# Axial attention on one Trainium2 core: maxima and scores on opposite 64 rows of the array, with the PSUM banks dealt out anew

## The reference, cut to what matters

```python
q = (x @ Wq).reshape(b, n, N_HEADS, HEAD_DIM)
k, v = jnp.split(ctx @ Wkv, 2, axis=-1)
...
q = apply_axial_rope(q, pos_map)
k = apply_axial_rope(k, ctx_pos_map)
scale = 1.0 / np.sqrt(HEAD_DIM).astype(np.float32)
logits = jnp.einsum('bqhd,bkhd->bhqk', q, k) * scale
w = jax.nn.softmax(logits, axis=-1)
attn = jnp.einsum('bhqk,bkhd->bqhd', w, v)
attn = attn.reshape(b, n, N_HEADS * HEAD_DIM)
return attn @ Wout + bout
```

## Time and profile before

| | |
|---|---|
| Median of 3 runs | 2910.94 us (2908.63 to 2911.35) |
| The profiled execution | 2908.72 us |
| Its span, first to last instruction | 2906.9 us |
| PE, DVE, ACT, POOL busy | 85%, 62%, 43%, 10% |
| Mean granted TensorE clock | 0.951 of full |
| First and last maxima of the stage | 2023.1 and 2585.3 us |

### The profile page before, as it was taken

How to read it: one execution, slowest core, us unless ns; L and a number is a source line. 1 busy time by engine, 2 the same in 40 slices (tenths; PEclk the granted TensorE clock), 3 DMA queues, 4 the chain that set the end, 5 groups by cost and what they waited for, 6 DMA issues and landing times. The chain is left out here.

```text
span 2906.9 us, 42566 instructions
## 1 busy us (share of the span) xinstructions
PE 2467.0 (85%) x15730; PEld 1904.7 (66%) x15746; DVE 1799.7 (62%) x5199; ACT 1248.9 (43%) x2982; POOL 297.7 (10%) x535
## 2 busy tenths in 40 slices
PE   5889999999974999799999999995888888883674
PEld 4668999998864999476667766763655555551332
DVE  6656767667875666445445544454566666657986
ACT  3434445444433211244344434452544444436663
POOL 3211100001000000000000000002111111101220
PEclk8999999999986999999999999997999999996887
DMA  4101211112005000000000000001000000003001
GB/s 156 62 23 41 70 37 40 69 36 74 29 26 194 1 1 1 1 1 1 1 1 1 1 1 1 1 1 51 5 5 5 5 5 5 5 1 133 1 1 58
DMA packets 41212, 83.41 MB, mean 29 GB/s; under 512 B 4528, under 2 KB 17840, under 8 KB 39856
## 3 DMA queue, kind: packets, MB, share of 16 engines
q1 hardware_dynamic: 41008, 80.70, 7.9%
HBM read 72.30 MB, written 8.39 MB: 28 GB/s over the span
## 5 line engine op out<-in xcount | busy, mean ns | idle before, releaser
L1990 DVE TENSOR_REDUCE s_nmax<-s_a_ps 128x2 f32<-128x512 f32 x256 | 174.3, 686 | 198.7 <-PE s_a_ps L1772 195.7
L651 ACT ACTIVATE s_p<-s_ms,s_nmax 128x256 f32<-128x256 f32 x256 | 128.5, 503 | 192.3 <-DVE s_nmax L754 192.3
L754 DVE CUSTOM_DVE_ANT_0 s_ms<-s_s_ps,s_bias 128x256 f32<-128x256 f32 x256 | 98.2, 421 | 175.9 <-PE s_s_ps L529 175.5
L1375 ACT ACTIVATE l_wo_w<-l_wo_w,s_nmax 128x128 f32<-128x128 f32 (+1 forms) x256 | 114.4, 447 | 197.8 <-DVE s_nmax L1471 197.0
L512 PE MATMUL s_q_ps<-s_xT,s_wh 128*128 128x256 f32 x1024 | 189.6, 286 | 0.0
L1215 PE MATMUL s_s_ps<-l_wqb_w,s_lT 128*128 128x512 f32 x384 | 175.7, 597 | 16.0 <-DVE l_wo_w L1441 15.3
L914 PE MATMUL s_h_ps<-s_xh,s_t 128*128 128x256 f32 x704 | 173.0, 284 | 9.3 <-DVE s_xl L1002 9.3
L1886 ACT ACTIVATE s_pT<-s_s_ps 128x512 f32<-128x512 f32 x256 | 151.6, 606 | 59.6 <-PE s_s_ps L1785 57.3
L562 PE MATMUL s_y_ps<-s_wh,s_oT 128*128 128x512 f32 x512 | 173.0, 399 | 0.0
L914 PE MATMUL s_h_ps<-s_xl,s_t 128*128 128x256 f32 x704 | 172.4, 283 | 0.0
L512 PEld LDWEIGHTS s_q_ps<-s_xT,s_wh 128*128 128x128 f32 x1024 | 165.5, 193 | 6.0 <-issue 0.5
(11 more groups left out here) (304 smaller groups left out, 6686.8 us busy)
## 6 DMA issues: line engine op xcount, KB each, us to landing
s_x_raw<-kept SPq DMA_DIRECT2D x24, 512.0 KB, 3.3
s_c_in<-in_ctx_T SPq DMA_DIRECT2D x32, 256.0 KB, 2.5
l_wqb_w<-in_l_xwq SPq DMA_DIRECT2D x4, 1024.0 KB, 7.8
l_wqb_w<-in_l_xwo SPq DMA_DIRECT2D x4, 1024.0 KB, 10.1
kept<-s_x_raw SPq DMA_DIRECT2D x8, 512.0 KB, 2.7
l_wo_w<-in_l_wo SPq DMA_DIRECT2D x1, 4096.0 KB, 15.5
s_raw<-in_l_w1T SPq DMA_DIRECT2D x2, 2048.0 KB, 9.9
s_raw<-in_l_w2T SPq DMA_DIRECT2D x2, 2048.0 KB, 21.5
```

The lines of the kernel that those rows point to most:

```text
L651: act.activation(p[:, h % PR, q, :], ms[:, h % 2, q, :], ACT.Exp, scale=-1.0, bias=nmax[:, h % PR, q:q + 1], accum_out=den[:, h % PR, q:q ...
L754: dve.tensor_tensor_reduce(ms[:, h % 2, q, :], s_ps[:, h % 2, q * S:(q + 1) * S], bias[:, h // PER % B, :], -SCALE, 3.0e38, ALU.add, ALU.m ...
L1375: act.activation(p[:, h % PR, q, 0:(q + 1) * P], ms[:, h % 2, q, 0:(q + 1) * P], ACT.Exp, scale=-1.0, bias=nmax[:, h % PR, q:q + 1], accum ...
L1990: dve.tensor_reduce(nmax[:, g % 2, :, 2 * pair + e], a_ps[:, n % 2, :].rearrange("p (q k) -> p q k", q=QT), AX_X, ALU.max, negate=True).th ...
```

## The change

The maxima of head n and the scores of head n-11 are now issued in turns, part by part, in `products`, each on the 64 rows in which its head lies. `head_of` puts heads of even number in the upper and of odd number in the lower half, so that the two heads of a step always lie in opposite halves. `kTz` becomes `kT` without the zeros; the two fills go away, and a k is copied out by one instruction. Transpositions follow the products. `t_ps` has one bank, `a_ps` three. `outputs` works on a whole group of eight heads, in steps 5, 13, 21 and 29, ahead of the step's projection, and `pT` holds sixteen heads. The projections move: q from steps 10 and 14 to 8 and 11, v from 12 and 13 to 15 and 16, y from 16 and 18 to 18 and 20; k stays at 19 and 21. The reciprocal moves from step 21 to 22 (and each eighth from there), the scaling from 22 to 23.

```diff
     LAG = GH + 3
-    QUADS = H // 4
-    QUAD_LAG = LAG + 3 + 2
-    OUT_LAG = QUAD_LAG + 5
-    Q_AT, K_AT, V_AT, Y_AT = (10, 14), (19, 21), (12, 13), (16, 18)
+    PV_LAG = LAG + GH + 2
+    OUT_LAG = PV_LAG + 1
+    Q_AT, K_AT, V_AT, Y_AT = (8, 11), (19, 21), (15, 16), (18, 20)
...
-        return n // GH, n % 4, n % GH // 4
+        return n // GH, n % GH // 2, n % 2
...
-        kTz = m.sb("kTz", [P, H, S], F32R)
+        kT = m.sb("kT", [P, H // 2, S], F32R)
...
-        pT = m.sb("pT", [P, GH, QT, S])
+        pT = m.sb("pT", [P, 2 * GH, QT, S])
...
-        t_ps = m.ps("t", [P, 2, 512])
+        t_ps = m.ps("t", [P, 512])
-        a_ps = m.ps("a", [P, 2, 512])
+        a_ps = m.ps("a", [P, 3, 512])
...
-                pe.wait_ge(t_out, at + 1)
+                pe.wait_ge(t_out, at + 2)
...
-                pe.wait_ge(a_out, b * H + n + 1)
-                for q in range(QT):
-                    mm = pe.matmul(a_ps[:, n % 2, q * S:(q + 1) * S], qTx[:, g % 2, pair, q * P:(q + 1) * P],
-                                   kTz[:, GH * g + 2 * pair + e, :], start=True, stop=True)
-                mm.then_inc(a_full, 1)
+                pe.wait_ge(a_out, max(b * H + n, 1))
...
+            def products(b, n, j):
+                for part in range(QT):
+                    if n is not None:
+                        g, pair, e = head_of(n)
+                        rows = slice(XD * e, XD * (e + 1))
+                        mm = pe.matmul(a_ps[:, (b * H + n) % 3, part * S:(part + 1) * S], qTx[rows, g % 2, pair, part * P:(part + 1) * P],
+                                       kT[rows, PAIRS * g + pair, :], start=True, stop=True)
+                        if part == QT - 1:
+                            mm.then_inc(a_full, 1)
+                    if j is not None:
+                        g, pair, e = head_of(j)
+                        rows = slice(XD * e, XD * (e + 1))
+                        mm = pe.matmul(s_ps[:, j % 2, part * S:(part + 1) * S], kT[rows, PAIRS * g + pair, part * P:(part + 1) * P],
+                                       qTm[rows, g % 2, pair, :], start=True, stop=True)
+                        if part == QT - 1:
+                            mm.then_inc(s_full, 1)
+
+            def outputs(b, g):
+                pe.wait_ge(s_out, b * H + 2 + GH * (g + 1))
+                pe.wait_ge(o_out, b * G + g + 1)
+                for e in range(2):
+                    for k in range(QT):
+                        for part in range(2):
+                            for pair in range(PAIRS):
...
             def steps_of(b):
                 for n in range(H):
+                    whose = "prev" if n < LAG else "here"
+                    if has(b, whose):
+                        scores_wait(b, whose, (n - LAG) % H)
                     if has(b, "here"):
-                        greatest(b, n)
+                        greatest_wait(b, n)
+                    products(b, n if has(b, "here") else None, (n - LAG) % H if has(b, whose) else None)
                     for use in t_turns.steps[n]:
...
-                    heads = slice(GH * g, GH * (g + 1), 2)
-                    act.copy(kTz[0:XD, heads, cols], t[0:XD])
-                    heads = slice(GH * g + 1, GH * (g + 1), 2)
-                    act.copy(kTz[XD:P, heads, cols], t[XD:P]).then_inc(t_out, 1)
+                    act.copy(kT[:, PAIRS * g:PAIRS * (g + 1), cols], t).then_inc(t_out, 1)
...
-            act.copy(kTz[0:XD, 1::2, :], blank[0:XD, :].unsqueeze(1).broadcast_to([XD, H // 2, S])).then_inc(fixed, 1)
...
-            dve.tensor_copy(kTz[XD:P, 0::2, :], blank[XD:P, :].unsqueeze(1).broadcast_to([XD, H // 2, S])).then_inc(fixed, 1)
```

More of the change, by code:

```diff
@@ L1726, in rows_over @@
                     pe.wait_ge(x_full, b * G + g + 1)
-                pe.wait_ge(t_out, at + 1)
+                pe.wait_ge(t_out, at + 2)
                 for k in range(4):
-                    to = t_ps[:, bank, k * P:(k + 1) * P]
+                    to = t_ps[:, k * P:(k + 1) * P]
                     if of == "x":
@@ L1768, in greatest, with scores_wait @@
                         pe.wait_ge(t_out, t_turns.at(b - 1, last) + 3)
[L1770 to L1776 removed]
+                pe.wait_ge(a_out, max(b * H + n, 1))
+            def scores_wait(b, whose, n):
                 g, pair, e = head_of(n)
@@ L1783, in scores @@
                 pe.wait_ge(s_out, (b + shift[whose]) * H + n + 1)
-                for k in range(QT):
-                    mm = pe.matmul(s_ps[:, n % 2, k * S:(k + 1) * S], kTz[:, GH * g + 2 * pair + e, k * P:(k + 1) * P],
-                                   qTm[:, g % 2, pair, :], start=True, stop=True)
-                mm.then_inc(s_full, 1)
-            def outputs(b, m):
-                g, e = m // 2, m % 2
-                pe.wait_ge(s_out, b * H + 2 + 4 * m + 4)
-                if e == 0:
-                    pe.wait_ge(o_out, b * G + g + 1)
-                for k in range(QT):
-                    for part in range(2):
-                        for pair in range(PAIRS):
-                            ones_or_values = one[:, e, :] if part else v[:, k, GH * g + 2 * pair + e, :]
-                            mm = pe.matmul(o_ps[32 * pair:32 * pair + 32, part, :], ones_or_values,
-                                           pT[:, 4 * e + pair, k, :], start=(e == 0 and k == 0 and part == 0),
-                                           stop=(e == 1 and k == QT - 1 and part == 1))
+            def products(b, n, j):
[14 more added lines that the diff above has]
+                            mm.then_inc(s_full, 1)
@@ new lines, in outputs @@
+            def outputs(b, g):
[5 more added lines that the diff above has]
+                            for pair in range(PAIRS):
+                                ones_or_values = one[:, e, :] if part else v[:, k, GH * g + 2 * pair + e, :]
+                                mm = pe.matmul(o_ps[32 * pair:32 * pair + 32, part, :], ones_or_values,
+                                               pT[:, GH * (g % 2) + 2 * pair + e, k, :],
+                                               start=(e == 0 and k == 0 and part == 0),
+                                               stop=(e == 1 and k == QT - 1 and part == 1))
@@ L1815, in steps_of @@
                             rows_over(b + shift[use[0]], t_turns.at(b, use), t_turns.bank(b, use), *use[1:])
-                    whose = "prev" if n < LAG else "here"
-                    if has(b, whose):
-                        scores(b, whose, (n - LAG) % H)
-                    whose = "prev" if n < QUAD_LAG else "here"
-                    if n % 4 == QUAD_LAG % 4 and has(b, whose):
-                        if whose == "here" and n == QUAD_LAG:
+                    whose = "prev" if n < PV_LAG else "here"
+                    if n % GH == PV_LAG % GH and has(b, whose):
+                        if whose == "here" and n == PV_LAG:
                             pe.wait_ge(f_out, f_turns.at(b, ("here", "v", QT - 1)) + 2)
-                        outputs(b + shift[whose], (n - QUAD_LAG) % H // 4)
+                        outputs(b + shift[whose], (n - PV_LAG) % H // GH)
                     for use in f_turns.steps[n]:
@@ L1854, in _ @@
                            ACT.Sin).then_inc(sines, 1)
-            act.wait_ge(fixed, 1)
-            act.copy(kTz[0:XD, 1::2, :], blank[0:XD, :].unsqueeze(1).broadcast_to([XD, H // 2, S])).then_inc(fixed, 1)
             def rows_over(at, bank, of, g, q):
                 act.wait_ge(t_full, at + 1)
-                t = t_ps[:, bank, :].rearrange("p (k n) -> p k n", k=4)
+                t = t_ps[:, :].rearrange("p (k n) -> p k n", k=4)
                 cols = slice(q * P, (q + 1) * P)
@@ L1989, in greatest @@
                 dve.wait_ge(a_full, b * H + n + 1)
-                dve.tensor_reduce(nmax[:, g % 2, :, 2 * pair + e], a_ps[:, n % 2, :].rearrange("p (q k) -> p q k", q=QT),
+                dve.tensor_reduce(nmax[:, g % 2, :, 2 * pair + e], a_ps[:, (b * H + n) % 3, :].rearrange("p (q k) -> p q k", q=QT),
                                   AX_X, ALU.max, negate=True).then_inc(a_out, 1)
```

20 lines of the change are left out of this document (9 added, 11 removed).

## The result

The changed kernel takes 3022.65 us (median of 4 runs, 3021.59 to 3027.71) against 2911.14 for the kernel before (2908.63 to 2919.92). The ratio is 1.0381 [1.0356, 1.0406]: it is 111 us slower where I had forecast 34 slower, and outside the range. The profiled execution has a span of 3019.8 us (before 2906.9) and a mean granted clock of 0.919 (before 0.951).

What follows compares the result with a forecast made beforehand. Waits decide, as neither PE nor DVE is full: steps 1 to 21 follow PE, the rest DVE. Six full batches by +5.0 give 30, the rest 4.3: +34 on 2908.72 is 2943, median 2945 us, range 2930 to 2962.

Steps and rivals of the forecast that it cites:

- Ahead of m25: Before step 25's transposition of maxima, which needs all eight maxima, PE would stand about 4.4 us because DVE is late.
- The three waits at f_ps: With moved projections, PE waits for DVE to empty the one f_ps bank: 2.35 at step 16, 1.1 at 19, 1.85 at 20.
- the one bank: Single transposes bank: a transposition starts 1.23 us after the last, costing 0.49 between neighbouring steps; +5.3 a batch in all.
- The 0.87 that I gave for x itself: Time for x's transposition, float32 in two passes, taken alike on PE and on the way out.
- Part B: From step 22 to step 1's transposition a batch follows DVE's chain: 20.9 us before, 20.7 after, so -0.2.
- part A: Steps 1 to 21, where a batch follows PE: 53.8 us before, and +5.2 after the change.
- I take 0.10, twice in most steps.: Price in us of each change between 64-row products and all else, bounded by 0 and 0.12; some 47 switches make 4.7.
- rival (1): Halves give no gain, because they don't overlap or loads queue: +18, so 2963 us; chance 0.18.
- A clock loss is possible ... I add nothing, at most 1 a batch.: In step 24's hole the granted clock falls in some batches, but PE waits for DVE there anyway: 0 added.
- +2.7 a batch for the projections' move: Waits at f_ps in part A sum to 5.3 after the move, where 2.6 stood before.
- -1.3 for the reductions that it hides: Query projection at step 8 hides the reciprocal and reduction for which PE waits about 1.3 us in step 7.
- +1.3 for the outputs as whole groups at the end: Last group whole behind the last exponential: 3.44 instead of 1.72, less 0.4 of earlier start, before the output projection.

Runs made afterwards that it cites:

- rows_only: The kernel before with maxima and scores on 64 rows in turns ahead of the transpositions; banks, outputs and projections as before: 2952.76 us, 1.0133.
- rows_in_place: The kernel before in its old order, with every product on its 64 rows and both matmuls of a pair in the same half: 2969.84 us, 1.0192.
- full_rows_2: The changed kernel with products on 128 rows again, two copies of k, `pT` of eleven heads and single-buffered rotation temporaries: 3045.86 us, 1.0446.
- order_only: The kernel before on 128 rows with only the new order in a step, both products and then transposes: 2928.34 us, 1.0049.
- filler: The changed kernel with products on data that nobody reads put into PE's holes in steps 25 and 1 to 4: 3009.63 us, 1.0324.
- two_t_f_old: The changed kernel with two banks for transposes, two for maxima, and the projections in their old steps: 3053.72 us, 1.0476.
- f_old: The changed kernel with the projections in the steps of before (q 10 and 14, v 12 and 13, y 16 and 18): 3050.42 us, 1.0478.
- two_t: The changed kernel with two banks of transposes and two of maxima again: 3007.6 us, 1.0321.
- rows_one_t: The kernel before with 64-row products in turns ahead of transpositions, plus one bank of transposes and three of maxima: 3008.72 us, 1.0318.
- split_cols: The changed kernel with each product of 256 columns split into two halves of 128 with the same weights: 3057.26 us, 1.051.

## Why the prediction was wrong

**What held.** Side by side: the two products of a round start within 0.01 us. The waits for s_nmax and s_oT vanish and nothing is paid out for them. A second product on the other half costs nothing beside the first, as I had it. Ahead of m25 PE stands and DVE's chain goes on; I had 4.4 us, the row has 3.1:

```profile
2433.45 0.75 PE L1734 MATMUL s_t_ps<-s_identr,s_qx 128*128 128x128 f32 x4 [3.11 <-DVE s_qx L1994]
```

The three waits at f_ps came at 1.8, 1.0 and 1.7 us (forecast 2.35, 1.1, 1.85). A transposition waits 0.34 for the one bank and starts 1.30 behind the last (2390.63 to 2391.93; forecast 0.49 and 1.23), and x waits 0.77 (forecast 0.9). The 0.87 that I gave for x itself stands in no row: in before it is 0.60 (0.90 from 2308.85 to 2309.75, less 0.30 for the transposition of k ahead of it), and as it is the same before and after, the forecast does not hang on it. Part B is 22.2 us (forecast 20.7), part A, up to product 22, about 66.5 (forecast 59.0).

**The step that failed first: "I take 0.10, twice in most steps."** This is the price of a change between 64-row products and all else, on which the gain of the overlap hung. Timeline of PE in steps 12 and 13 of after:

```profile
2390.20 0.38 PE L1786 MATMUL s_a_ps<-s_kT,s_qTx 64*128 64x256 f32 x1
...
2390.63 0.54 PE L1734 MATMUL s_t_ps<-s_identr,s_kx 128*128 128x128 f32 x4
2391.10 0.38 PE L1786 MATMUL s_a_ps<-s_kT,s_qTx 64*128 64x256 f32 x1
```

From the first round to the transposition it is 0.43, from there to the next product 0.47. I had 0.34 (0.24 and a switch) and 0.40 (0.30 and a switch). A step of products and one transposition takes 0.90, where I had 0.74; before it takes 0.84 to 0.95. At the lower level a round takes 0.38 (2363.38 to 2363.76 below). Taken apart: the 0.24 for two rounds side by side is what two distances inside a run would be; the first distance of a run is 0.10 longer, the one to the transposition 0.09 longer, and the transposition takes 0.47 for 0.30. That is 0.36 for the two changes of a step, where I had 0.20. With 47 changes in part A the difference is an estimated 3.8 us a batch, so that PE's work in A rises by 2.9 where I had it fall by 0.9.

The rows of before held most of this. I read a change only from the distance ahead of it (0.09 and 0.12 at the strips) and missed that the first distance behind it is longer too: a pair of maxima behind outputs takes 0.34 on the whole array, not 0.24 (2244.68 to 2245.02). This first distance is 0.22 in rows_only, rows_in_place and after, and on the whole array behind outputs as well (2302.58 to 2302.80 in full_rows_2); behind a transposition the whole array has 0.18 (order_only). What the 64 rows add of their own is some 0.03 there, 0.09 ahead of the transposition and 0.17 in it, against 0.24 that the overlap saves.

In size this is close to rival (1), but its mechanism is not what the runs show: the halves overlap. The Trainium skill (TensorE: Matmul & The Clock Gate, Part 3: Packing small matmuls) says that a weight load overlaps a matmul under way only when it goes to other rows. By that rule every round on the same rows would show its load. The trace disagrees, and the measurement decides: in rows_only the load at 2241.07 goes to the 64 rows on which the scores have just started, and the next product starts 0.12 later, at the pace of the stream.

What the half rows do to the whole kernel is rows_only less order_only: 24 us lost, of which a part may be the clock, lower in rows_only.

**"A clock loss is possible ... I add nothing, at most 1 a batch."** The second failure. Not one hole of 4 us but a batch full of holes of 0.7 to 3 us brings PE down to 1.2 GHz for 27.3 us of 88.7. It happens around the hole of m25, through steps 1 to 5, where the waits stand closest, and for 3.4 us in the middle of the batch. In step 5 outputs, which follow no wait at all, cost nearly double. Timeline of the outputs of step 5 in after, half of them at either level:

```profile
2371.47 1.08 PE L1809 MATMUL s_o_ps<-s_pT,s_v 128*32 128x256 f32 x8
...
2375.29 0.60 PE L1809 MATMUL s_o_ps<-s_pT,s_one 128*32 128x256 f32 x8
```

Eight records take 0.85 and 0.43 from start to start. In the first batch it is the same: the windows of 2030 to 2040 us have a clock of 0.50 in after and 1.00 in before, and that batch, where I had forecast 0.5 more, takes 12.4 more. That the clock is a cause and no bystander is shown by filler, which has more work and ends 13 us earlier. It is no more than a part: filler takes the time at 1.2 GHz from 27.3 to 10 us, but only 3.4 off a batch.

**Waits that the walk through the steps missed.** With the new order, a step's products stand ahead of its transposition, so the first scores of a group (step 3, 11, 19, 27) wait for the copy of the transposition just before, 0.7 us each time. Timeline of PE in step 3 of after:

```profile
2363.38 0.58 PE L1786 MATMUL s_a_ps<-s_kT,s_qTx 64*128 64x256 f32 x1 [0.68 <-ACT s_qTm L1877]
...
2365.62 1.09 PE L1731 MATMUL s_t_ps<-ident,s_xs 128*128 128x128 f32 x4 [0.77 <-ACT s_kT L1875]
```

Maxima now also wait for the exponentials of scores: a PE that puts both products into one round waits for both their banks. These are 32.5 us in the stage (16.3 and 16.2 in the waits above). Before the change the transpositions stood between the two products. order_only, which has the new order alone, is 14 us slower.

**The one bank.** Its term was +5.3 a batch and 40 in all. PE's waits for copies out of t_ps come to 18.7 us in the stage, less than half of it; the rest may lie in the missed waits, which now take the same time. What the bank costs hangs on what surrounds it: with the third bank of maxima that it pays for, it is 56 us put onto rows_only, 15 taken off the changed kernel, and nothing between two_t_f_old and f_old (1.0476 against 1.0478).

**The outputs and the projections.** I had added +2.7 a batch for the projections' move, -1.3 for the reductions that it hides and +1.3 for the outputs as whole groups at the end, and no wait of their own for the outputs. The runs have it the other way round. Whole groups (with the new `head_of`) cost 101 us with two banks of transposes and 42 with one. The projections' move takes back 46 of those with two banks (two_t against two_t_f_old) and 28 with one (after against f_old). I priced the projections against the waits of before instead of against what the outputs do to the old steps: y at 16 would wait 3 us for s_oT.

Six kernels with half rows and the new order differ only in these three parts:

| transposes, maxima | outputs | projections | kernel | ratio | a batch, us | of it at 1.2 GHz |
|---|---|---|---|---|---|---|
| 2, 2 banks | half groups | old | rows_only | 1.0133 | 78.9 | 11 |
| 1, 3 banks | half groups | old | rows_one_t | 1.0318 | 85.4 | 20.6 |
| 2, 2 banks | whole groups | old | two_t_f_old | 1.0476 | 92.2 | 27.4 |
| 1, 3 banks | whole groups | old | f_old | 1.0478 | 92.2 | 30.8 |
| 2, 2 banks | whole groups | new | two_t | 1.0321 | 85.4 | 20.5 |
| 1, 3 banks | whole groups | new | after | 1.0381 | 88.7 | 27.2 |

The batch is the mean of five, from the transposition of x in one to that in the next. The parts do not add up one by one, so each order of adding them gives another split. Along one path: order 14, half rows 24, one bank 56, and outputs with projections together 14 to 18. Along the other: order and rows 39, outputs 101, projections -46, the bank 15 to 18. Both end at some 110. The batches also bunch at a few lengths: 85.3 to 85.4 in rows_one_t, two_t and filler, 92.0 to 92.2 in f_old, two_t_f_old, full_rows_2 and split_cols. One step between them, 3.4 us, is 20 us in six batches, more than some of the differences that I read as the price of a part. Why the batches take these lengths no run shows.

What is shown: the half rows, the order, the bank and the outputs together cost the 111 us; the order (14 us) and the half rows (24) cost something by themselves; the outputs are a loss in both pairs of kernels and the projections' move a gain in both; the bank is a loss in two of three pairs. What stays open is how much of 111 us is the clock beyond 13, and what of the outputs' 42 to 101 us is their length in one step and what the low clock it meets there: no run holds one of these still.

## What to carry to other kernels

Two products on opposite halves of the array overlap, but here every two rounds stand between two changes to whole-array work, and the changes cost more than the overlap gives: read the price of a change on both sides of it, the last distance ahead and the first distance behind, and make the runs of half-row work long before counting on two at once. Before putting two products behind one another's waits, write down for both what they wait for, since the pair waits for the later. Where a change cuts PE's work into more short holes, expect the lower clock in the dense work behind them as well as in the holes, and look at windows of the granted clock at once. And when parts of a change are priced one at a time, measure one part in two surroundings: here the same bank cost 56, 15 and 0 us.

## What was not expected of the hardware

Two pairs of 64x256 on opposite rows take 0.43 us until the transposition behind them, and so does one pair alone. Four such matmuls on the same rows follow each other after 0.22, 0.12 and 0.12 (rows_only); on 128 rows behind outputs the distances are the same, but there the transposition follows after 0.12 and takes 0.30, while behind 64 rows it follows after 0.20 and takes 0.47.

In rows_in_place the first maxima of a step start at 2243.04, beside the first scores of the step before and ahead of its second scores at 2243.26, though both scores stand ahead of them in the program: on the other half this matmul did not wait for its turn.

8.2 of the 27.3 us at 1.2 GHz lie in dense work behind the holes: in after the stretch 2366.60 to 2377.10 has PE busy for 9.65 of 10.50 us at a mean clock of 0.61. Adding useless products made the whole kernel 13 us faster; adding still more gave 9 of them back.
